# Product with the values: every second round, two units in a row, instead of every round

## The chip, the cores and the metric

The kernel runs on one core of one Trainium2 chip. The metric is the device time of one execution in microseconds. TensorE (PE) does the matrix products and loads their weights (PEld), VectorE (DVE) reduces and copies, ScalarE (ACT) does the exponentials and copies, GpSimd (POOL) does elementwise work in SBUF only, and SyncE (SP) starts DMAs. Products land in PSUM, which has eight banks of 128 x 512 f32.

## The reference

One transformer block with adaptive layer norm, for 2048 tokens of 256 features: latent attention with 16 heads, then eight experts of which each token uses two. Cut to the part that matters here:

```python
q = _rms_norm(x @ w_qa, q_a_norm_w) @ w_qb                 # 16 heads of 128 + 64
c_kv, k_rope = kv[..., :64], kv[..., 64:]                  # latent keys and values
scores = einsum('bhsd,bhtd->bhst', q_full, k_full) * scale
scores = where(tril, scores, min)
attn = softmax(scores)
out = einsum('bhst,bhtd->bhsd', attn, v)                   # the product with the values
x = x + ga * (out @ w_o)
h = _layernorm(x) * (1 + cb) + sb
x = x + gb * experts(h)                                    # top 2 of 8
```

## The kernel before

The program has three stages: `prepare` (weights, keys, latent values), `attend` (attention) and `experts`. The change is in `attend` alone.

**Tiling.** An *item* is one head and one group of 512 query rows (16 heads x 4 groups = 64 items). Group g sees g+1 blocks of 512 keys. A *unit* is two key tiles of 128 of one item. An item of group g has 2g full units and then two diagonal ones: the first (`d` = 0, an even unit number) and the second (`d` = 2, an odd number), of which only the part under the diagonal is computed. Every item has an even number of units and so starts at an even one. There are 320 units; 96 of the odd ones are full, 64 are diagonal. Of each pair of heads the groups come in the order 3, 1, 2, 0, so that the pattern of the work repeats every 40 units.

**Banks.** Scores of a unit go to one of two pairs of banks (`s_pair`), turn by turn. Three banks (`work_bank`) take, turn by turn, the small jobs of `WORK_ORDER`: row maxima of the scores ("max", L849, read by DVE in L782 or L779), the spread of an item's maxima over all partitions ("shift", L856, read by ACT in L706), and three query products for each pair of items ("q", parts 0 to 2, L837, read by ACT in L692 and by DVE in L757 to L770). A job waits until the one three before it has been read. One bank (`o_bank`) collects the product with the values of an item, and DVE copies it out once for each item (L808).

**Order.** Every engine has the same loop over rounds, r = -13 to 321, written out by hand, and does its instructions strictly in that order. Semaphores are all that ties the engines together. In round r:

- PE: scores of unit r (L876, six f32 products, with two bf16 mask products L867 ahead of them on a diagonal unit) with the maxima of later items between the halves (L849), then a shift (L856) in some odd rounds, a query product (L837) in some, and then the product with the values, `weigh(r - 2)`: up to 24 small 16-bit products (L891, L893, L895).
- ACT: exponentials of unit r (L726, or L730 twice on a diagonal one), a shift copy, the *seed* of unit r+2 (L717: the shift written to the scores' banks, on which the scores accumulate), a query copy (L692), or in part 2 the query's high part (L699), which waits for DVE's sums.
- DVE: maxima, an item's maximum and its spread (L787, L792), the turn of the queries (L757 to L770), the seed of the second diagonal unit (L800), and the copy of an item's output (L808).
- POOL: the low part of the exponentials (L669, L675), and of the queries (L661).

The scores of unit r wait for its seed, and the seed for the exponentials of unit r-2, which had the same banks. The exponentials of unit u wait until unit u-4 has been weighed, since `pt` has four slots. The first unit of an item waits in `weigh` for the copy of the item before (`o_seen`).

Of the kernel before, what the change touches and what calls it, by code (L numbers as in the profile page):

```python
# [56 lines left out]
UNITS = []  # L57
# [48 lines left out]
def seen_by(n):  # L106

    use = WORK_ORDER[n]
    return {"max": "v", "shift": "a", "q": "va"}[use[0]] if use[0] != "q" or use[2] < 2 else ""


SEEN = {e: [0, *itertools.accumulate(e in seen_by(n) for n in range(len(WORK_ORDER)))] for e in "av"}


def live(u, half):
# [5 lines left out]
def seed_on_vector(u):  # L121

    return UNITS[u][2] == 2
# [452 lines left out]
def attend(nc, sb, sem, k):  # L576
# [7 lines left out]
    with ExitStack() as own:  # L584
# [32 lines left out]
        def wait_seen(eng, n):  # L617
# [4 lines left out]
            for e in seen_by(n):  # L622
                eng.wait_ge(work_seen[e], SEEN[e][n + 1])

# [5 lines left out]
        with nc.Block() as block:  # L630
# [116 lines left out]
            def _(dve):  # L747
# [25 lines left out]
                def maximum(c):  # L773
                    item, t, part, n = CHUNKS[c]
                    w = WORK[("max", c)]
                    dve.wait_ge(work_done, w + 1)
                    of, to = work_of(w)[:, 0:n * P], mx[:, item % MAXIMA, t, part:part + 1]
                    if part == ITEMS[item][1]:
                        dve.tensor_tensor_reduce(out=of, in0=of, in1=mask16[:, BW - n * P:], scale=1.0, scalar=LOWEST, op0=ALU.add,  # L779
                                                 op1=ALU.max, accum_out=to).then_inc(work_seen["v"], 1)  # L780
                    else:
                        dve.tensor_reduce(out=to, in_=of, axis=AXX, op=ALU.max).then_inc(work_seen["v"], 1)  # L782
# [20 lines left out]
                def evacuate(u):  # L803
                    item, _, d = UNITS[u]
                    hp, g, h = ITEMS[item]
                    head = 2 * hp + h
                    dve.wait_ge(pv_done, u + 1)
                    dve.tensor_copy(lat[:, BT * g:BT * g + BT, head * (KVL + 1):head * (KVL + 1) + KVL + 1],  # L808
                                    o_bank[:, 0:BT * (KVL + 1)].rearrange("p (t n) -> p t n", t=BT)).then_inc(o_seen, 1)

                for r in ROUNDS:
                    for c in CHUNKS_AT[r]:
                        maximum(c)
                    if r in ITEM_MAX_AT:
                        item_shift(ITEM_MAX_AT[r])
                    p, part = PREP_AT.get(r, (0, 4))
                    if part < 3:
                        query_turn(p, part)
                    if 0 <= r + 2 < NU and seed_on_vector(r + 2):
                        seed(r + 2)  # L820
                    if r >= 2 and UNITS[r - 2][2] == 2:
                        evacuate(r - 2)

            @block.tensor
            def _(pe):
# [53 lines left out]
                def weigh(u):  # L879
                    item, j, d = UNITS[u]  # L880
                    at = u % PT_RING
                    if u == FIRST_UNIT[item] and item > 0:
                        pe.wait_ge(o_seen, item)
                    for half in range(2):
                        pe.wait_ge(low_ok, OPS[u + 1] - (0 if d is None or half else 1))
                        for t in range(0 if d is None else d + half, BT):
                            to = o_bank[:, t * (KVL + 1):t * (KVL + 1) + KVL + 1]
                            mine = slice(t * P, t * P + P)
                            end = d is not None and t == d + half
                            low_values, with_one = values[:, j + half, 0:KVL], values[:, j + half, KVL:2 * KVL + 1]  # L890
                            pe.matmul(to, cut(pt[:, at, half, mine]), with_one, start=(u == FIRST_UNIT[item] and half == 0 and t == 0),  # L891
                                      stop=False, skip_group_check=True)
                            pe.matmul(to[:, 0:KVL], cut(pt[:, at, half, mine]), low_values, start=False, stop=False,  # L893
                                      skip_group_check=True)
                            last = pe.matmul(to, pt_lo[:, at, half, mine], with_one, start=False, stop=end, skip_group_check=True)  # L895
                    last.then_inc(pv_done, 1)
# [6 lines left out]
                for r in ROUNDS:  # L903
                    for half in range(2):
                        if 0 <= r < NU:
                            scores(r, half)
                        for c in chunks_at(r, half):
                            maximum(c)
                    if r in SHIFT_AT:
                        shift_rows(SHIFT_AT[r])  # L910
                    p, part = PREP_AT.get(r, (0, 3))
                    if part < 3:
                        query_products(p, part)
                    if r >= 2:
                        weigh(r - 2)


def cut(a):

    return a.bitcast(BF16).rearrange("p (n e) -> p n e", e=2)[:, :, 1]  # L920
# [512 lines left out]
```

## Time and profile before

| | |
|---|---|
| median of 3 runs | 1254.86 us (1247.85 to 1255.21) |
| profiled execution | 1254.86 us, span 1253.1 us |
| attention in it | from about 116 to 991 us of the span |
| busy share of the span | PE 91%, PEld 77%, DVE 68%, ACT 63%, POOL 55% |
| mean granted TensorE clock | 0.956 |

PE is the busiest engine and the chain that ended last runs over it. Its busy time in the profile is modelled, since matmuls overlap: what one costs is read from the distance between two starts, not from its duration. The granted clock was 1.0 from 146 to 992 us of the span, nearly the whole of the attention.

### The profile page before, as it was taken

Reading aid. Unit: us, or ns where it says so; the run is one execution under the profiler, and the core shown is the slowest. Engines: PE = TensorE matmul, PEld = TensorE weight load, DVE = VectorE, ACT = ScalarE, POOL = GpSimd, SP = SyncE. Lnnn points to the kernel's source line nnn. Section 1 sums busy time; section 2 is a strip of 40 time slices with the busy share of each in tenths; the row PEclk is TensorE's granted clock in tenths of the full one; section 3 lists DMA queues with packets and bytes.
Section 4 is the critical chain, followed back from the end, with each engine's and each line's share of the span. In section 5 each row is a group of like instructions: output and inputs, shape, how many; then the busy total and the mean of one; then the engine's idle time right before and its main releaser. Section 6 shows DMA issues by size and latency. Waiting matters only on the chain. (4 is left out here: it accounts for less than half of the span.)

```text
span 1253.1 us, 27841 instructions
## 1 busy us (share of the span) xinstructions
PE 1146.3 (91%) x11372; PEld 958.8 (77%) x11372; DVE 846.8 (68%) x1900; ACT 787.5 (63%) x1166; POOL 690.3 (55%) x569
## 2 busy tenths in 40 slices
PE   2856899999999999999999999999999778989897
PEld 1744577888888888888888888888887667888886
DVE  2632876677676776777777677776675576767676
ACT  1254577777777878777787787877777532322222
POOL 0022366777777768686787776877777711202000
PEclk9876699999999999999999999999999879989998
DMA  9301110000100200100020020010000310000000
GB/s 277 95 1 48 29 44 18 2 18 25 38 19 2 62 2 19 44 19 19 2 62 18 2 61 2 19 44 19 18 2 1 114 57 1 1 18 1 18 18 17
DMA packets 57695, 39.91 MB, mean 32 GB/s; under 512 B 7744, under 2 KB 57152, under 8 KB 57408
## 3 DMA queue, kind: packets, MB, share of 16 engines
q1 hardware_dynamic: 51216, 33.94, 9.2%
q10 hardware_dynamic: 6352, 4.19, 1.4%
q8 instruction: 90, 1.47, 0.5%
q14 instruction: 37, 0.30, 0.1%
HBM read 33.66 MB, written 4.46 MB: 30 GB/s over the span
## 5 line engine op out<-in xcount | busy, mean ns | idle before, releaser
L669 POOL TENSOR_TENSOR pt_lo<-pt 128x1024 f16<-128x1024 f32 x192 | 370.5, 1939 | 181.5 <-ACT pt L726 181.2
L782 DVE TENSOR_REDUCE gates<-bank 128x1 f32<-128x512 f32 x384 | 261.6, 689 | 148.0 <-PE bank L849 145.1
L717 ACT ACTIVATE pair<-shift 128x1024 f32<-128x1024 f32 x256 | 263.7, 1030 | 12.2 <-ACT pt L730 0.4
L726 ACT ACTIVATE pt<-pair 128x1024 f32<-128x1024 f32 x192 | 196.2, 1022 | 108.3 <-PE pair L876 107.7
L891 PEld LDWEIGHTS bank<-values,pt 128*128 128x128 bf16 x2176 | 196.8, 98 | 80.1 <-issue 52.6
L891 PE MATMUL bank<-values,pt 128*128 128x65 f16 x2176 | 235.2, 194 | 6.0 <-DVE lat L808 5.1
L893 PE MATMUL bank<-values,pt 128*128 128x64 f16 x2176 | 231.8, 192 | 0.0
L895 PE MATMUL bank<-values,pt_lo 128*128 128x65 f16 x2176 | 230.8, 194 | 0.0
L675 POOL TENSOR_TENSOR pt_lo<-pt 128x512 f16<-128x512 f32 (+3 forms) x256 | 178.3, 722 | 45.0 <-ACT pt L730 44.9
L893 PEld LDWEIGHTS bank<-values,pt 128*128 128x128 bf16 x2176 | 202.0, 98 | 0.0
L895 PEld LDWEIGHTS bank<-values,pt_lo 128*128 128x128 f16 x2176 | 201.3, 97 | 0.0
L779 DVE CUSTOM_DVE_ANT_0 bank<-bank,mask 128x128 f32<-128x128 f32 (+3 forms) x256 | 126.1, 498 | 53.8 <-PE bank L849 48.7
L730 ACT ACTIVATE pt<-pair 128x512 f32<-128x512 f32 (+3 forms) x256 | 110.4, 437 | 45.7 <-PE pair L876 32.1
L876 PE MATMUL pair<-q_hi,kt_a_hi 128*128 128x512 f32 (+1 forms) x320 | 131.1, 410 | 0.0
L876 PE MATMUL pair<-q_hi,kt_b_hi 128*128 128x512 f32 (+1 forms) x320 | 130.5, 408 | 0.0
L849 PE MATMUL bank<-kt_a_hi,q_hi 128*128 128x512 f32 (+2 forms) x320 | 118.6, 375 | 3.4 <-DVE qf L757 1.6
L849 PE MATMUL bank<-kt_b_hi,q_hi 128*128 128x512 f32 (+2 forms) x320 | 117.4, 369 | 0.7 <-DVE gates L779 0.6
L876 PE MATMUL pair<-q_lo,kt_a_hi 128*128 128x512 f32 (+1 forms) x320 | 117.2, 366 | 0.0
L876 PE MATMUL pair<-q_hi,kt_a_lo 128*128 128x512 f32 (+1 forms) x320 | 117.2, 366 | 0.0
L876 PE MATMUL pair<-q_hi,kt_b_lo 128*128 128x512 f32 (+1 forms) x320 | 117.1, 366 | 0.0
L876 PE MATMUL pair<-q_lo,kt_b_hi 128*128 128x512 f32 (+1 forms) x320 | 116.6, 364 | 0.0
L661 POOL TENSOR_TENSOR q_lo<-qf,q_hi 128x512 fp32r<-128x512 f32 x64 | 84.4, 1340 | 19.6 <-ACT q_hi L699 18.1
(218 smaller groups left out, 2380.0 us busy)
## 6 DMA issues: line engine op xcount, KB each, us to landing
turn_by<-rope_cos_by_feature SPq DMA_DIRECT2D x64, 128.0 KB, 3.0
turn_by<-rope_sin_by_feature SPq DMA_DIRECT2D x64, 128.0 KB, 3.0
xs<-in_L_attn_x ACTq DMA_DIRECT2D x1, 2048.0 KB, 25.5
lat<-in_L_attn_w_o SPq DMA_DIRECT2D x1, 2048.0 KB, 26.6
xs_again<-in_L_attn_x SPq DMA_DIRECT2D x1, 2048.0 KB, 8.1
out<-xs_again SPq DMA_DIRECT2D x4, 512.0 KB, 2.8
lat<-in_L_wmod SPq DMA_DIRECT2D x1, 1536.0 KB, 16.3
lat<-in_L_attn_w_qb SPq DMA_DIRECT2D x1, 1152.0 KB, 8.0
```

The source lines that it names most:

```text
L669: pool.tensor_tensor(out=pt_lo[:, at].rearrange("p a n -> p (a n)"), in0=full, in1=cut(full), op=ALU.subtract).then_inc(low_ok, 1)
L675: pool.tensor_tensor(out=pt_lo[:, at, half, live(u, half):], in0=full, in1=cut(full), op=ALU.subtract).then_inc(low_ok, 1)
L717: act.activation(s_pair[u % 2][:, :, :], shift[:, item % SHIFTS:item % SHIFTS + 1, :].to_broadcast([P, 2, BW]), ACT.Copy).then_inc(seeded[ ...
L726: act.activation(pt[:, at], s_pair[u % 2][:, :, :], ACT.Exp).then_inc(exp_done, 1)
L730: act.activation(pt[:, at, half, live(u, half):], s_pair[u % 2][:, half, live(u, half):], ACT.Exp).then_inc(exp_done, 1)
L779: dve.tensor_tensor_reduce(out=of, in0=of, in1=mask16[:, BW - n * P:], scale=1.0, scalar=LOWEST, op0=ALU.add, op1=ALU.max, accum_out=to).t ...
L782: dve.tensor_reduce(out=to, in_=of, axis=AXX, op=ALU.max).then_inc(work_seen["v"], 1)
L849: pe.matmul(work_of(w)[:, 0:cols], q, kt_hi[h][:, part * BW:part * BW + cols], start=True, stop=True).then_inc(work_done, 1)
L876: last = pe.matmul(to, keys[a], q[b], start=False, stop=(m == 2), skip_group_check=True)
L891: pe.matmul(to, cut(pt[:, at, half, mine]), with_one, start=(u == FIRST_UNIT[item] and half == 0 and t == 0), stop=False, skip_group_check ...
L893: pe.matmul(to[:, 0:KVL], cut(pt[:, at, half, mine]), low_values, start=False, stop=False, skip_group_check=True)
L895: last = pe.matmul(to, pt_lo[:, at, half, mine], with_one, start=False, stop=end, skip_group_check=True)
```

## The change

`weigh` is no longer called once in every round. Even rounds have none; an odd round r has two in a row, of units r-3 and r-2. So an odd unit is weighed in the round in which it was weighed before, and an even unit one round later. DVE's copy of an item's output belongs to the odd units and stays in its round. The same instructions run, on the same banks: three for the small jobs, one for the output.

```diff
+def values_due(r):
+
+    return (r - 3, r - 2) if r >= 3 and r % 2 else ()
...
             @block.vector
...
-                    if r >= 2 and UNITS[r - 2][2] == 2:
-                        evacuate(r - 2)
+                    for u in values_due(r):
+                        if UNITS[u][2] == 2:
+                            evacuate(u)
...
             @block.tensor
...
-                    if r >= 2:
-                        weigh(r - 2)
+                    for u in values_due(r):
+                        weigh(u)
```

PE at the end of an even round that holds a query product, and what follows it (a line number of the changed kernel is 6 higher than the same line before). Before:

```order
2453 L837 MATMUL bank<-ql_hi,wq_pair_hi 128x512 [waits work_seen_a,wq_in]
2454 L837 MATMUL bank<-ql_lo,wq_pair_hi 128x512
2455 L837 MATMUL bank<-ql_hi,wq_pair_lo 128x512
2456 L891 MATMUL bank<-values,pt 128x65 [waits low_ok,o_seen]
2457 L893 MATMUL bank<-values,pt 128x64
2458 L895 MATMUL bank<-values,pt_lo 128x65
2459 L891 MATMUL bank<-values,pt 128x65
```

In the changed kernel, at the same place:

```order
2453 L843 MATMUL bank<-ql_hi,wq_pair_hi 128x512 [waits work_seen_a,wq_in]
2454 L843 MATMUL bank<-ql_lo,wq_pair_hi 128x512
2455 L843 MATMUL bank<-ql_hi,wq_pair_lo 128x512
2456 L873 MATMUL pair<-ident,mask 128x128 [waits seeded_v]
2457 L873 MATMUL pair<-ident,mask 128x128
2458 L882 MATMUL pair<-q_hi,kt_b_hi 128x256
```

The 21 value products (L891, L893, L895) that stood between the query product and the next unit's scores are gone from there; the odd round's scores, its maxima and its own query product come that much sooner after the even round's. They stand, with the 9 of the odd unit behind them, after the odd round's query product:

```order
2466 L843 MATMUL bank<-ql_hi,wq_pair_hi 128x512 [waits work_seen_a,work_seen_v]
2467 L843 MATMUL bank<-ql_lo,wq_pair_hi 128x512
2468 L843 MATMUL bank<-ql_hi,wq_pair_lo 128x512
2469 L897 MATMUL bank<-values,pt 128x65 [waits low_ok,o_seen]
2470 L899 MATMUL bank<-values,pt 128x64
2471 L901 MATMUL bank<-values,pt_lo 128x65
```

The second place is the start of an odd full unit, three rounds behind another query product (a part 2). Before, its first product follows value products:

```order
2829 L891 MATMUL bank<-values,pt 128x65
2830 L893 MATMUL bank<-values,pt 128x64
2831 L895 MATMUL bank<-values,pt_lo 128x65
2832 L876 MATMUL pair<-q_hi,kt_b_hi 128x512 [waits seeded_a]
2833 L876 MATMUL pair<-q_lo,kt_b_hi 128x512
```

In the changed kernel it follows a maximum, and nothing stands between it and the even round's jobs:

```order
2806 L882 MATMUL pair<-q_hi,kt_b_lo 128x512
2807 L855 MATMUL bank<-kt_b_hi,q_hi 128x384 [waits work_seen_v]
2808 L882 MATMUL pair<-q_hi,kt_b_hi 128x512 [waits seeded_a]
2809 L882 MATMUL pair<-q_lo,kt_b_hi 128x512
```

What moved in both is only the block of value products; the order of all else on PE is as it was.

## Rows read from the trace of the kernel before

**Rows 1.** The page, part 1: busy time, share of the span, instructions

```profile
PE 1146.3 (91%) x11372; PEld 958.8 (77%) x11372; DVE 846.8 (68%) x1900; ACT 787.5 (63%) x1166; POOL 690.3 (55%) x569
```

**Rows 2.** Stretches, us: busy us (instructions) of PE, PEld, DVE, ACT, POOL; clock; DMA

```profile
146.00:200.00 54.00, 51.21 (x541) 41.23 (x540) 42.62 (x90) 39.95 (x56) 36.62 (x34) 1.00 0.09 26
200.00:942.00 742.00, 741.48 (x8542) 610.96 (x8543) 532.27 (x1126) 587.92 (x777) 551.57 (x443) 1.00 0.08 23
942.00:990.00 48.00, 43.21 (x560) 35.86 (x558) 26.29 (x51) 33.75 (x50) 35.04 (x32) 1.00 0.01 1
```

**Rows 3.** Timeline, PE around the value products of a full unit: start us, duration us

```profile
495.33 0.40 PE L849 MATMUL bank<-kt_b_hi,q_hi 128*128 128x512 f32 x1
...
495.56 0.21 PE L891 MATMUL bank<-values,pt 128*128 128x65 f16 x1
...
496.31 0.47 PE L876 MATMUL pair<-q_hi,kt_b_hi 128*128 128x512 f32 x1
...
496.62 0.39 PE L876 MATMUL pair<-q_lo,kt_b_hi 128*128 128x512 f32 x1
```

**Rows 4.** Groups, 200 to 950 us: count | busy us, mean ns | idle before

```profile
L891 PE MATMUL bank<-values,pt 128*128 128x65 f16 x1948 | 210.4, 194 | 2.0 <-DVE lat L808 1.6
...
L699 ACT ACTIVATE q_hi<-qf 128x512 fp32r<-128x512 f32 x54 | 34.1, 633 | 9.8 <-DVE qf L770 9.2
```

**Rows 5.** Waits of PEld, 200 to 950 us: total us, times, longest us

```profile
PEld bank L891 <- DVE lat L808: 4.6, 8, 2.0
```

**Rows 6.** Waits of PE, 942 to 990 us

```profile
PE bank L891 <- DVE lat L808: 3.6, 3, 1.8
PE pair L867 <- DVE pair L800: 1.0, 1, 1.0
```

**Rows 7.** Timeline from a query product 0 to part 1

```profile
408.25 0.21 PE L891 MATMUL bank<-values,pt 128*128 128x65 f16 x1
...
408.99 0.27 PE L867 MATMUL pair<-ident,mask 128*128 128x128 bf16 x2
...
409.05 0.58 ACT L692 ACTIVATE qf<-bank 64x512 f32<-64x512 f32 x1
...
410.20 0.39 PE L837 MATMUL bank<-ql_hi,wq_pair_hi 96*128 96x512 f32 x1
```

**Rows 8.** Timeline from a query product 2 to the shift behind it

```profile
414.17 0.21 PE L891 MATMUL bank<-values,pt 128*128 128x65 f16 x1
...
414.82 0.48 PE L876 MATMUL pair<-q_hi,kt_b_hi 128*128 128x512 f32 x1
...
415.20 1.41 DVE L770 TENSOR_TENSOR qf<-bank,qf 64x512 f32<-64x512 f32 x2
...
416.75 0.41 PE L856 MATMUL bank<-spread,ones_r 128*128 128x512 f32 x1
```

**Rows 9.** Timeline: a query part 2 on ACT, the seed behind it

```profile
382.55 0.21 PE L891 MATMUL bank<-values,pt 128*128 128x65 f16 x1
...
383.20 0.48 PE L876 MATMUL pair<-q_hi,kt_b_hi 128*128 128x512 f32 x1
...
384.36 1.29 ACT L699 ACTIVATE q_hi<-qf 128x512 fp32r<-128x512 f32 x2 [0.29 <-DVE qf L770]
...
385.56 1.01 ACT L726 ACTIVATE pt<-pair 128x1024 f32<-128x1024 f32 x1
...
386.60 1.03 ACT L717 ACTIVATE pair<-shift 128x1024 f32<-128x1024 f32 x1
...
387.19 0.21 PE L891 MATMUL bank<-values,pt 128*128 128x65 f16 x1
...
387.93 0.48 PE L876 MATMUL pair<-q_hi,kt_b_hi 128*128 128x512 f32 x1
```

**Rows 10.** Timeline: a seed on ACT and its unit, at another place of the pattern

```profile
429.78 1.03 ACT L717 ACTIVATE pair<-shift 128x1024 f32<-128x1024 f32 x1
...
431.23 0.48 PE L876 MATMUL pair<-q_hi,kt_a_hi 128*128 128x512 f32 x1
```

## The prediction

> **What bounds the kernel now.** I read the busy shares first, then the stretches, the waits of PE, and last the timeline around the places where the change moves work. PE is busiest with 91% [rows 1], but its durations overlap. The stretches say more: from 200 to 942 us, three fifths of the span, PE is busy for 741.48 of 742 us at a granted clock of 1.00, which is the upper of its two levels, 2.4 GHz; ACT is busy for 79% of it, POOL for 74%, DVE for 72% [rows 2]. So PE sets the pace there with hardly a wait, and the others follow with some slack. What the change is worth is what it does to PE's row of starts: something taken out of it is gained, any wait put into it is lost in full.
>
> **The change, part by part.**
>
> *Fewer changes between f32 and 16-bit products.* Around a block of 24 value products the starts are: a maximum at 495.33, the first value product at 495.56, the next unit's scores at 496.31 and 496.62 [rows 3]. An f32 product of 512 columns holds up the next start by 0.23 us. The first one behind the block holds the next up for 0.31 us, so leaving the block costs 0.08 us. The block takes 0.75 us; its 24 products at the 194 ns of their group [rows 4] would make 4.7 us, so durations say nothing, and the pitch is about 31 ns. The start of the block is slow by some 0.03 us (I take the later products of the block at 30 ns: 24 x 30 is 0.72). Each separate block thus costs 0.11 us. Where is one saved? An odd full unit now follows a maximum or a query product, f32 behind f32: 96 times. At the 64 odd diagonal units it is not: their two bf16 mask products stand first, so there was one 16-bit run from the value products to the masks, and now there are the masks alone with the same change on either side. 96 x 0.11 = **10.5 us less**.
>
> *The copy of the output.* The first value product of an item waits until DVE has copied the item before. From 200 to 950 us the weight loads waited for it 8 times, 4.6 us in all, of which the loads would have waited about 0.2 each for their turn: 3 us [rows 5], 1.6 of it shown at the product itself [rows 4]. At the end of the attention, where little else fills PE, it is 3.6 us in 3 waits, and 1.0 us for a seed [rows 6]. The pair of units never straddles two items, and between the last of an item and the first of the next stand now the scores of two units, not of one, some 2 us more: longer than the longest wait, 2.0. I take the 3 us as gained and half of the 4.6 us at the end, since the same late DVE delays a seed or a query there next: **5.3 us less** (bounds: 0 and 7.6).
>
> *What the moved block used to cover.* This is the other side. In an even round the block gave ACT and DVE 0.65 to 0.75 us (21 or 24 products) between the even round's jobs and the odd unit. ACT's and DVE's work of the even round starts when PE's scores and jobs of that round are done, and does not come sooner; PE's odd unit does, by the block and, if full, by the 0.08 us. Two rounds together are as long as before, so what depends on the odd round two back keeps its distance, and what even rounds need from odd ones gains room. Losses are only where odd work needs something of the even round before it (or three before), with less slack than 0.65 to 0.83 us. From the timeline, with 0.06 us for a semaphore (an estimate between 0.03, from 386.57 to 386.60 on one engine [rows 9], and 0.14, from 416.61 to 416.75 [rows 8]):
>
> 1. Query product 1 waits until the bank of product 0 is read. ACT's copy ends at 409.05 + 0.58 = 409.63; product 1 starts at 410.20 [rows 7]. It would start 0.74 us sooner (408.99 - 408.25), at 409.46, and waits until 409.69: 0.23 us. The other three places of the pattern have 0 to 0.1 us more slack; mean 0.17. There are 27 preparations of queries from 200 to 950 us (54 high parts, two for each [rows 4]): 4.6 us.
> 2. The shift that follows a query part 2 needs DVE's sums: these end at 415.20 + 1.41 = 416.61, the shift starts at 416.75 [rows 8]. It would start 0.65 + 0.08 us sooner, at 416.02: 0.65 us of wait. This meets one preparation in four: 4.4 us.
> 3. The seed behind a part 2 is the dear one. ACT has to do the high parts (384.36 to 385.6), the exponentials of the odd unit (385.56), and only then the seed of the odd unit after it, 386.60 + 1.03 = 387.63; that unit starts at 387.93 [rows 9]. In the changed order its start lies one block and one change earlier (the block at 387.19 to 387.93 comes behind it, and the change at 383.20 is gone): 387.93 - 0.74 - 0.08 = 387.11 against 387.69, a wait of 0.6 us. At two more places of the pattern the seed ends at 429.78 + 1.03 = 430.81 for a start at 431.23 [rows 10], 0.42 us of slack instead of 0.30, and the wait is 0.46; the fourth has an odd diagonal unit there, whose seed is DVE's and has slack. Mean 0.51 at three of four preparations, 20 times: 10.3 us.
>
> Together **19.3 us more**. Bounds: 0, if ACT and DVE had been held up by PE's odd rounds more than I read; and twice as much, 39 us, if each wait makes the next engine late again.
>
> *Before 200 us.* Here DVE has three maxima in most rounds and PE is busy for 51.21 of 54 us [rows 2]. In the six odd rounds the jobs come 0.7 us sooner to a DVE that is already late: between 0 and 4 us more. I take **1 us**, near the lower end, since DVE itself loses nothing. The clock is 1.00 from 146 us on; the block moved before that changes a round or two.
>
> *POOL, DMAs, DVE's order.* No DMA moves. Value products of even units come a round later, those of odd units at the same place, so POOL's low parts are never later than needed. The exponentials of unit u wait for the value products of u-4: these now stand at the end of the odd round before, ahead of the scores that the exponentials need anyway. Nothing added.
>
> Sum: -10.5 - 5.3 + 19.3 + 1 = +4.5 us. The profiled execution took 1254.86 us, 1.8 us over its span, and is itself the median of the three: **1259 us**. The three runs lie within 0.6%, so I count less than 1% (12.5 us) as no change that could be told.
>
> **A rule weighed against the trace.** The rows put a load and its value product at 31 ns, in runs of at most 26 with the masks. The Trainium skill (TensorE: Matmul & The Clock Gate, Back-to-back issue gap) gives about 81 ns for each load with its product of 128 columns in a sustained stream. This trace does not agree for its 65 columns: a block of 24 would take 1.9 us, and took 0.75. By the page's figure every wait above would grow by some 1.2 us, and 54 of them would make the sum about +69 us, an estimate from that page that I do not use.
>
> **The rivals.**
>
> - *The waits do not appear* (0.17). For it: ACT and DVE are busy for under 80%, and an odd round gives back what an even one takes. Against: the three chains hang on even rounds and were followed instruction by instruction. Then -10.5 - 5.3: 1239 us.
> - *The lateness carries on* (0.13). For it: ACT has 0.6 us of slack in a mean round (154 us [rows 2] over some 270 rounds, ten for each preparation), and the high parts alone take 1.3. A late seed makes late exponentials, a late shift, and a late seed again. Against: the odd round is 0.7 us longer than it was and lets ACT catch up. Twice the waits: 1259 + 19 = 1278 us, slower. It decides from 28 us of waits on, 1.4 times my sum, where the slowdown passes 1%.
> - *Long runs of small products starve* (0.08). PE now does 48 loads and products in a row at 96 places; the longest run in these rows is 26. All that is shown is that the supply of instructions makes 742 us / 8542 = 87 ns for a pair on average [rows 2] and 31 ns in short runs, for which a stock may have been filled during the long f32 products. If it could do only the average, the 22 pairs beyond 26 cost 22 x 56 ns = 1.2 us each time: +118 us, 1377 us; anything between is possible. The Trainium skill (the same page, its table) has a queue of 64 for TensorE, 32 pairs, by which 16 pairs would run dry: 86 us instead of 118 if the supply had only that average. No row here shows a queue's depth.
> - *Part of the waits* (0.10): half of them, 1249 us.
>
> My forecast has 0.52: its own range, from the bounds of the single terms, is 1250 to 1268.
>
> **How the numbers follow.** Faster by over 1% needs under 1242.3: the first rival and a little of the fourth, 0.18. Slower by over 1% needs over 1267.4: the second and third rival and 0.04 of the forecast's own range, 0.25. Within 1%: 0.57. The range reaches from the first rival to the second, 1236 to 1279, and leaves out the starving one, half of the second and a third of the first: 0.2.
>
> **What would show it.** Right: 96 of the 0.31 us distances behind 16-bit products are gone; PE's starts show waits for ACT's seed (L717) before odd full units three rounds behind a query part 2, for DVE's sums before a shift, and short ones before query product 1; the waits for L808 are gone; and PE's busy share from 200 to 942 us falls from 99.9% to about 97.5%. Wrong: if the distance between value products grows in the second half of a run of 48, the third rival holds; if no wait of PE shows at these places and the stretch to 942 us ends more than 5 us sooner, the waits did not come; if DVE or ACT have waits on each other in rounds without a query, lateness carries on.

## The result, and the profile after

| | before | changed |
|---|---|---|
| median, us (8 runs each) | 1254.58 | 1261.17 |
| lowest to highest, us | 1247.85 to 1256.13 | 1258.15 to 1265.1 |
| profiled execution: time, span, us | 1254.86, 1253.1 | 1260.55, 1258.8 |

The ratio is 1.0064 [1.0042, 1.0086]: slower by 0.6%, or 6.6 us, less than the 1% that the prediction counted as no change. Forecast were 1259 us, in a range of 1236 to 1279.

The page of the changed kernel, part 1, and then its stretches (columns as in [rows 2]). Lines of PE stand 6 further down than before, those of the other engines 5: the scores are L882, the value products L897 to L901, the shift L862, the query products L843, ACT's seed L722, its high parts L704, DVE's query sums L775, its copy of the output L813.

```profile
PE 1144.1 (91%) x11372; PEld 959.2 (76%) x11372; DVE 859.0 (68%) x1900; ACT 772.5 (61%) x1166; POOL 700.7 (56%) x569
```

```profile
146.00:200.00 54.00, 52.48 (x561) 42.99 (x561) 43.64 (x93) 39.98 (x56) 38.44 (x33) 1.00 0.09 26
200.00:942.00 742.00, 727.69 (x8320) 601.17 (x8317) 534.98 (x1097) 562.42 (x761) 549.41 (x433) 1.00 0.08 22
942.00:990.00 48.00, 47.28 (x581) 39.70 (x580) 32.06 (x70) 37.46 (x50) 36.44 (x30) 1.00 0.01 2
```

Beside [rows 1] nothing shows: all shares are within 2 points. Beside [rows 2] it does. In the long stretch PE was busy for 741.48 of 742 us and is now for 727.69: 98.1% against 99.9%, and 8320 products fit where 8542 did. Before 200 us and behind 942 us it is busier than it was (52.48 for 51.21, 47.28 for 43.21 us; the attention now ends 10 us later, so the last window holds somewhat other work). The waits of PE from 200 to 942 us name the cause (line <- what it waited for: us in all, times, longest):

```profile
PE pair L882 <- ACT pair L722: 8.2, 20, 0.5
PE bank L862 <- DVE qf L775: 2.9, 6, 0.5
PE bank L843 <- DVE qf L762: 0.7, 2, 0.4
PE bank L843 <- DVE gates L787: 0.4, 1, 0.4
```

These are the places of the forecast: 20 waits for a seed, 6 for the sums before a shift, and the three longest of those before query product 1. The view counts only gaps over 0.15 us, and counts them from the modelled end of the product before, so its sum of 12.2 us is too low; the distances between starts, below, give the full price and show a wait at all 27 query products 1. The wait for the copy of the output is gone from here. At the end of the attention, 942 to 1000 us, it is gone too; in place of 4.6 us in [rows 6] stand 0.7:

```profile
PE bank L897 <- POOL pt_lo L674: 0.4, 1, 0.4
PE pair L873 <- DVE pair L805: 0.3, 1, 0.3
```

One such wait closely, at the place of [rows 9]. First ACT and then PE of the changed kernel (start us, duration us):

```profile
385.69 1.29 ACT L704 ACTIVATE q_hi<-qf 128x512 fp32r<-128x512 f32 x2 [0.30 <-PE pair L882]
386.88 1.01 ACT L731 ACTIVATE pt<-pair 128x1024 f32<-128x1024 f32 x1
387.92 1.03 ACT L722 ACTIVATE pair<-shift 128x1024 f32<-128x1024 f32 x1
...
383.64 0.39 PE L843 MATMUL bank<-ql_hi,wq_pair_lo 96*128 96x512 f32 x1
383.87 0.40 PE L882 MATMUL pair<-q_hi,kt_b_hi 128*128 128x512 f32 x1
384.11 0.39 PE L882 MATMUL pair<-q_lo,kt_b_hi 128*128 128x512 f32 x1
...
388.24 0.34 PE L855 MATMUL bank<-kt_b_hi,q_hi 128*128 128x384 f32 x1
389.01 0.50 PE L882 MATMUL pair<-q_hi,kt_b_hi 128*128 128x512 f32 x1 [0.43 <-ACT pair L722]
389.35 0.39 PE L882 MATMUL pair<-q_lo,kt_b_hi 128*128 128x512 f32 x1
```

ACT still does high parts, exponentials and seed in this order, and the seed ends at 387.92 + 1.03 = 388.95. A maximum of 384 columns holds up the next start by 0.17 us, so the scores could have started at 388.41; they start at 389.01. The wait is 0.60 us, as forecast. Two more things are to be seen. At 383.87 the odd unit follows a query product, f32 behind f32, and the next start comes 0.24 us later and not 0.31: the saved change. And behind the wait the next start comes after 0.34 us and not 0.23: the wait costs 0.11 us more than itself. That was in no term.

### The profile page after: what moved, and what is told of

It is laid out like the page before. It is cut to its first block and busy times, and to the rows that moved or that the text cites. A ratio compares the mean times of both kernels' runs of the same rounds, so it can differ in the third digit from the quotient of the medians.

```text
span 1258.8 us, 27841 instructions
## 1 busy us (share of the span) xinstructions
PE 1144.1 (91%) x11372; PEld 959.2 (76%) x11372; DVE 859.0 (68%) x1900; ACT 772.5 (61%) x1166; POOL 700.7 (56%) x569
## 3 DMA queue, kind: packets, MB, share of 16 engines
q8 instruction: 90, 1.47, 0.5%
## 5 line engine op out<-in xcount | busy, mean ns | idle before, releaser
L787 DVE TENSOR_REDUCE gates<-bank 128x1 f32<-128x512 f32 x384 | 263.2, 690 | 138.0 <-PE bank L855 130.9
L722 ACT ACTIVATE pair<-shift 128x1024 f32<-128x1024 f32 x256 | 263.5, 1029 | 12.2 <-ACT pt L735 0.4
L897 PEld LDWEIGHTS bank<-values,pt 128*128 128x128 bf16 x2176 | 197.5, 98 | 35.3 <-issue 33.5
L897 PE MATMUL bank<-values,pt 128*128 128x65 f16 x2176 | 216.9, 193 | 0.9 <-DVE lat L813 0.5
L899 PE MATMUL bank<-values,pt 128*128 128x64 f16 x2176 | 215.2, 192 | 0.0
L901 PE MATMUL bank<-values,pt_lo 128*128 128x65 f16 x2176 | 214.6, 194 | 0.0
L680 POOL TENSOR_TENSOR pt_lo<-pt 128x512 f16<-128x512 f32 (+3 forms) x256 | 185.0, 747 | 53.0 <-ACT pt L735 52.4
L901 PEld LDWEIGHTS bank<-values,pt_lo 128*128 128x128 f16 x2176 | 199.8, 97 | 0.0
L735 ACT ACTIVATE pt<-pair 128x512 f32<-128x512 f32 (+3 forms) x256 | 103.5, 431 | 64.6 <-PE pair L882 59.5
L882 PE MATMUL pair<-q_hi,kt_a_hi 128*128 128x512 f32 (+1 forms) x320 | 128.6, 402 | 5.6 <-ACT pair L722 5.6
L882 PE MATMUL pair<-q_hi,kt_b_hi 128*128 128x512 f32 (+1 forms) x320 | 127.4, 398 | 2.6 <-ACT pair L722 2.6
L882 PE MATMUL pair<-q_hi,kt_a_lo 128*128 128x512 f32 (+1 forms) x320 | 117.4, 367 | 0.0
L882 PE MATMUL pair<-q_lo,kt_a_hi 128*128 128x512 f32 (+1 forms) x320 | 117.1, 366 | 0.0
L882 PE MATMUL pair<-q_hi,kt_b_lo 128*128 128x512 f32 (+1 forms) x320 | 117.1, 366 | 0.0
L882 PE MATMUL pair<-q_lo,kt_b_hi 128*128 128x512 f32 (+1 forms) x320 | 116.7, 365 | 0.0
```

The lines of the kernel that those rows point to most:

```text
L680: pool.tensor_tensor(out=pt_lo[:, at, half, live(u, half):], in0=full, in1=cut(full), op=ALU.subtract).then_inc(low_ok, 1)
L722: act.activation(s_pair[u % 2][:, :, :], shift[:, item % SHIFTS:item % SHIFTS + 1, :].to_broadcast([P, 2, BW]), ACT.Copy).then_inc(seeded[ ...
L735: act.activation(pt[:, at, half, live(u, half):], s_pair[u % 2][:, half, live(u, half):], ACT.Exp).then_inc(exp_done, 1)
L882: last = pe.matmul(to, keys[a], q[b], start=False, stop=(m == 2), skip_group_check=True)
```

## Where the time went

To add this up I took all starts of attention work on PE from unit 40 to unit 240, five patterns of 40 units, and split the distances: the 0.232 us of a product of 512 columns (0.174 for 384, 0.117 for 256, 0.03 for a value product); 0.085 for the first f32 product behind a 16-bit run; what lies inside a value block; and each distance over 0.05 us that is left, as a wait (with the slower start behind it). The 0.085 is a mean too: behind value products or masks the first product of 512 columns holds up the next start by 0.317 us in every kernel here, against 0.232. In us, all kernels of this document:

| kernel | total | changes to f32 | waits | unit 319 starts at | from there to the end |
|---|---|---|---|---|---|
| before | 528.5 | 17.0 (200) | 1.2 | 987.2 | 265.9 |
| changed | 543.2 | 11.9 (140) | 21.7 | 997.6 | 261.2 |
| e1, e2, e3 | 539.5, 535.7, 532.7 | 13.6, 11.9, 13.6 | 15.8, 14.2, 9.0 | 991.0, 988.5, 984.4 | 263.2, 266.4, 263.9 |
| e4, e5 | 535.1, 548.0 | 11.9, 17.0 | 13.6, 20.9 | 985.9, 1015.1 | 265.7, 263.4 |
| e6, e7 | 576.0, 579.2 | 34.0, 11.9 | 27.7, 55.9 | 1068.7, 1073.3 | 260.1, 265.8 |
| e8, e9 | 533.8, 525.2 | 13.2, 13.6 | 10.8, 1.7 | 987.2, 976.2 | 266.4, 266.5 |
| e10, e11, e12 | 535.5, 530.1, 523.3 | 11.9, 12.3, 12.3 | 13.9, 8.0, 1.3 | 986.3, 981.2, 972.4 | 265.9, 262.9, 266.2 |

From before to changed the 200 units took 14.7 us more: 20.5 more waits, 5.1 less for 60 changes and 1.3 less inside the blocks (together 0.107 us for each saved change; 0.6 us is left over). Up to unit 40 the changed kernel gains 2.0 us (252.1 and 250.1), behind unit 240 another 2.3 (206.6 and 204.3). So unit 319 starts 10.4 us later. Of the 2.0 us, 0.9 lie before the first unit (141.6 and 140.7 us), where no values are weighed yet; over all kernels here it starts between 139.1 and 142.5 us, so this is luck, and the attention itself costs 11.3 us. The rest of the program, which is the same code in both, took 4.7 us less, and that is no merit of the change. The stretches behind the attention, of before, of the changed kernel and of e9:

```profile
991.00:1253.10 262.10, 222.69 (x1376) 200.92 (x1376) 182.98 (x441) 75.09 (x119) 41.69 (x27) 0.91 0.09 29
```

```profile
1001.60:1258.80 257.20, 217.07 (x1376) 195.61 (x1376) 182.82 (x442) 75.14 (x119) 41.77 (x27) 0.94 0.09 29
```

```profile
980.20:1242.70 262.50, 222.71 (x1376) 201.00 (x1376) 182.99 (x442) 75.09 (x119) 41.74 (x27) 0.91 0.09 29
```

All three do the same 1376 products; DVE, ACT and POOL are busy for the same time to 0.2 us, and only PE is not. The column that differs is the granted clock, 0.94 against 0.91: PE was at the lower level, 1.2 GHz, for 31.7 us there, and for 49.0 (before) and 49.1 (e9). The runs of the changed kernel bear it out: five had a mean clock of 0.961 to 0.964 and took 1258.15 to 1261.8 us, three had 0.956 or 0.957, as before's profile, and took 1263.6 to 1265.1. Over the other kernels the end follows the clock too, but not it alone: it took 260.1 us with 28.2 us at the lower level (e6) and 266.5 with 49.1 (e9), yet 265.7 and 263.4 with 42.5 and 42.4 (e4, e5). With equal clocks the change thus costs 9 to 10 us, near what the attention says; the 6.6 of the medians hold some luck. For this reason the experiments are judged by the attention first.

## The experiments

My theory was: the block of value products gave three chains of ACT and DVE their cover, and each wait comes from the loss of one place of it. Against it stood that the waits come from lateness that is handed on (then putting one place back mends more than its place), and that PE loses something in long runs of small products. e1 to e4 and e7 to e12 start from the changed kernel, e5 and e6 from the one before. e1, e2, e3, e8 and e9 replace the rule of rounds by a table: units for which COND holds have their values in the round of before (one change to f32 more if the odd unit behind is a full one, none if it is diagonal), all others stay paired:

```
-    return (r - 3, r - 2) if r >= 3 and r % 2 else ()
+VALUES_ROUND = {u: u + 2 if u % 2 or COND else u + 3 for u in range(NU)}
+    return [u for u in (r - 3, r - 2) if VALUES_ROUND.get(u) == r]
```

### e1: the values put back in the round of a query part 2

```
COND: PREP_AT.get(u + 2, (0, 3))[1] == 2
```

> The changed kernel, but in the 32 even rounds that hold a query part 2 the value products stay as they were (one unit there, one in the odd round behind). My theory (waits of what hangs on even rounds): the waits for the seed three rounds behind a part 2 (0.47, 0.60 and 0.70 us per 40 units, with 0.11 each to start again) and the one before the shift (0.64 + 0.11) go, 2.85 us per 40 units; 4 of the 12 saved changes from 16-bit to f32 come back, 0.44 us. Net 2.4 us x 6.75 = 16 us less than the changed kernel: about 1245 us. Rival 1 (long runs of small products are slow by themselves): 27 of 96 runs of 48 are halved, so about a quarter of the 17 us of unexplained loss goes, 1257 us. Rival 2 (ACT and DVE are late everywhere once rounds are uneven): waits move to other rounds, no change, 1259 to 1261 us.

Measured: 1260.19 us, 1.0048 [1.0031, 1.0064] against before. The waits of PE, 200 to 942 us:

```profile
PE pair L885 <- ACT pair L725: 6.1, 19, 0.4
PE bank L846 <- DVE gates L790: 0.4, 1, 0.4
```

A miss, and it taught the geometry. The wait before the shift is gone (this block stands right ahead of it), but the seed waits are still there (0.37, 0.49 and 0.61 us at their three places, about 0.11 less than in the changed kernel, since the saved change came back). The seed that ACT does after the high parts belongs to the unit three rounds behind part 2, and the block that covered it is the one of the round before that unit, not that of part 2.

### e2 and e3: the values put back in the round of part 0, and of parts 0 and 2

```
COND of e2: PREP_AT.get(u + 2, (0, 3))[1] == 0
COND of e3: PREP_AT.get(u + 2, (0, 3))[1] in (0, 2)
```

> The changed kernel, but in the 32 even rounds that hold a query product 0 the value products stay as they were. My theory: the waits before query product 1 go (0.24, 0.28, 0.19 to 0.59, 0.27 us per 40 units, with 0.08 each to start again), 1.4 us per 40 units; no change from 16-bit to f32 comes back, since the odd unit behind each of these rounds is a diagonal one. 9 us less than the changed kernel: about 1252 us. Rival 1 (long runs): the pairs at these places are the short ones of diagonal units or of a full unit and a diagonal one, so nothing or 1 us. Rival 2 (lateness everywhere): no change.

> The changed kernel with the value products of one unit left in all 64 even rounds that hold a query part 0 or 2. If the two kinds of waits are apart, their gains add: 16 + 9 = 25 us less than the changed kernel, 1236 us, and 1.4% less than the kernel before: what is left of the change is 8 saved changes per 40 units (7 us in all) and the waits for the copy of the output that are gone (3 us, and up to 8 at the end of the attention). If lateness merely moves (rival 2): 1250 us or more, and waits for the seed at other places in the trace.

Measured: e2 1257.08 us, 1.0029 [1.0014, 1.0043]; e3 1252.22 us, 0.9988 [0.9976, 1.0001]. The waits of e2, and then those of e3:

```profile
PE pair L885 <- ACT pair L725: 8.2, 20, 0.6
PE bank L865 <- DVE qf L778: 2.9, 6, 0.5
```

```profile
PE pair L885 <- ACT pair L725: 6.1, 19, 0.4
```

Each block put back takes away its own wait: query product 1 in e2, that and the shift in e3. e2 gains what was forecast, 9.1 us in the attention (997.6 - 988.5; 9 were expected); in the time only 4, since its end is 5.2 us longer than the changed kernel's short one. e3 gains 13.2 of the 25 expected: the seeds keep their waits, some 12 us (0.37, 0.49 and 0.60 in 40 units, and the starts behind them, 6.75 times). No place mends another, which speaks against lateness that is handed on.

### e4 and e5: another distance of the preparations, with and without the pairing

```
-AHEAD, PREP_AHEAD = 5, 6
+AHEAD, PREP_AHEAD = 5, 5
```

> The changed kernel, with every preparation of queries one round later, so that parts 0 and 2 fall into odd rounds, which have two units of value products behind them, and part 1 into an even one. My theory: the waits for the seed and before query product 1 go (they hang on rounds that are long now), and a wait of 0.25 to 0.35 us comes before query product 2 or the shift in the same round, since these now hang on the even round of product 1: -29 + 9 us, 1241 us. Rival 2 (lateness everywhere): no change, 1261 us. A preparation that is one round later for its readers costs nothing if the first maxima of an item had more than 3 us of slack, and shows as a wait for q_hi if not.

> The kernel before, with every preparation of queries one round later: the control for the fourth run. In it all rounds have their value products, so nothing should depend on whether a query part is in an even or an odd round: no change by my theory, 1253 to 1257 us. If it were faster by itself, the gain of the fourth run would not be one of the pairing.

Measured: e4 1253.42 us, 0.9992 [0.9975, 1.001]; e5 1280.49 us, 1.0205 [1.0184, 1.0226]. The waits of e4, and then those of e5:

```profile
PE bank L843 <- ACT qf L697: 6.2, 20, 0.4
PE bank L862 <- issue: 1.4, 6, 0.2
PE pair L873 <- DVE pair L805: 1.3, 6, 0.2
```

```profile
PE bank L891 <- DVE lat L808: 23.1, 26, 1.6
PE pair L867 <- ACT pair L717: 2.1, 1, 2.1
```

With the jobs of queries moved by a round the seed waits are gone and waits before query product 2 stand in their place: the cost of the pairing sits where jobs and missing blocks meet, not in the pairing itself. e4 misses its 1241 us: its new waits (0.37 to 0.54 us before three of the four query products 2, 0.40 before a shift, 0.37 before a diagonal unit) come to 13.6 us in 200 units, where the 0.25 to 0.35 us of the forecast made 9 in the whole attention. The control e5 was expected to change nothing and is 26 us slower: it brings 26 waits for the copy of the output, which e4 does not have. So here the pairing is worth 27 us (1280.49 - 1253.42). 10.3 of it are the saved changes. The waits are the rest: counted in starts up to unit 319, e5 has 39.7 us, 31.9 of them for value products, and e4 has 23.0, none for value products. The term that the prediction sized at 5.3 is worth some 32 here: its size hangs on how late DVE is where an item ends.

### e6: more changes to f32, without moving anything across rounds

The block of before is cut in two: its first half follows the first chunk of scores' maxima of the same round, its second stays.

```
 for half in range(2):
     ...
+    if half == 0 and r >= 2:
+        weigh(r - 2, 0)
...
-weigh(r - 2)
+weigh(r - 2, 1)
```

> The kernel before, with the value products of each unit in two blocks, that of the first key tile between the two halves of the next scores and that of the second where all were: twice as many blocks, the same products. It measures what a change from f32 to 16-bit and back costs. My theory, 0.11 us for each additional block (0.08 to leave it, 0.03 to start it): 320 x 0.11 = 35 us more, 1290 us, and up to 5 more for waits on the copy of the output, which comes 1 us sooner. If changes cost nothing and the 0.31 us after a block were hidden elsewhere: no change.

Measured: 1330.75 us, 1.0625 [1.0594, 1.0655]; its waits are for L808 (23.2 us) and POOL's low parts (1.8 us). The table has the answer to what it was made for: 200 blocks more cost 17.0 us of changes and 2.3 within the blocks, 0.097 us each, against 0.107 saved by the change and 0.11 forecast. The time misses its 1290 us by 41 through the waits, of which at most 5 were expected. Of its 47.5 us more in that stretch 26.5 are waits: half of each block now comes a part of a round sooner, nearer to the copy of the output.

### e7: the pair in even rounds

```
-    return (r - 3, r - 2) if r >= 3 and r % 2 else ()
+    return [u for u in ((r - 3, r - 2) if r % 2 == 0 else (r - 2,) if r == NU + 1 else ()) if 0 <= u < NU]
```

> The changed kernel with the pairs in even rounds: units r-3 (odd) and r-2 (even) in an even round, so that the odd rounds are the short ones and each second pair or so straddles two items. My theory: the seeds and the first query product no longer wait (they hang on even rounds, now long); query product 2, or a shift, waits 0.3 us behind the odd round of product 1 (27 times, 8 us); the changes saved are those before even full units, 10.5 us; and at the 63 starts of an item the copy of the output stands between two blocks in a row with nothing to cover it, 0.42 us of copy and some 0.2 for the semaphores, 40 us, more where DVE is late. 1254.6 - 10.5 + 8 + 40 = 1292 us. If the copy's wait were hidden, 1252 us.

Measured: 1340.07 us, 1.0682 [1.0658, 1.0705]. Its only wait of PE from 200 to 942 us, and one case of it on DVE and PE:

```profile
PE bank L897 <- DVE lat L813: 56.8, 49, 2.9
...
501.02 0.42 DVE L813 COPY lat<-bank 128x260 f32<-128x260 f32 x1
...
501.50 0.20 PE L897 MATMUL bank<-values,pt 128*128 128x65 f16 x1 [0.83 <-DVE lat L813]
```

Now a pair straddles two items: its odd unit ends one, its even unit begins the next, and between them PE can do nothing but wait for the copy from the single output bank, 0.9 to 1.7 us and once 2.5 in a pattern. All waits for seeds, shifts and queries are gone, so the same saved changes come with other waits, two and a half times as long (55.9 us against 21.7 in 200 units). The forecast of 1292 us had the place right and the price too low: 0.6 us for each of 63 copies, 40 us, where the 62 waits up to unit 319 sum to 86. This is what the odd rounds of the change avoid.

### e8 and e9: the block ahead of the late seed put back, and all three places

```
COND of e8: PREP_AT.get(u, (0, 3))[1] == 2
COND of e9: that of e8, or that of e2, or (u + 3 in SHIFT_AT and that of e1)
```

> The first run left the waits for the seed where they were, because it put back the wrong block: a seed behind a query part 2 in round r is waited for by unit r+3, and what no longer stands ahead of that is the value block of unit r, in round r+2. Here that block, and no other, stays in its old round (32 of them). My theory: the three waits for the seed go (0.48, 0.60, 0.70 us per 40 units and 0.11 each to start again), three saved changes come back (0.3 us), all other waits stay: 1.8 us x 6.75 = 12 us less than the changed kernel, 1249 us. Two of the first units of items are among the blocks, so the 0.23 us for the copy of the output may be back once per 40 units. Rival (a late ACT shows wherever rounds are uneven): the waits for the seed move to another unit and the time stays at 1258 to 1261 us.

> The changed kernel with one value block left in its old round at each place where a wait was found: in rounds with a query product 0, in the round two behind a part 2, and in that of a part 2 with a shift behind it. My theory: no waits are left from unit 40 to 240 but 0.23 us per 40 units for the copy of the output, 8 of 12 changes stay saved: 3.7 us less per 40 units than the changed kernel, 25 us in all, 1236 us; 1.4% faster than the kernel before, where 7 us are the changes, and the rest the waits for the copy of the output and the end of the attention. Rival: 1250 us as in the third run.

Measured: e8 1254.35 us, 0.9999 [0.9991, 1.0008]; e9 1243.96 us, 0.9921 [0.9909, 0.9934]. The waits of e8, and then those of e9:

```profile
PE bank L865 <- DVE qf L778: 2.9, 6, 0.5
PE bank L900 <- DVE lat L816: 1.1, 6, 0.2
PE bank L846 <- DVE gates L790: 0.4, 1, 0.4
```

```profile
PE bank L900 <- DVE lat L816: 1.1, 6, 0.2
```

This settles the seed: with the right block put back all 20 waits are gone. e8 takes 9.4 us less than the changed kernel over 200 units (1.9 for 40, where 1.8 were expected). In e9 nearly everything is gone: over 200 units it takes 18.0 us less than the changed kernel (3.6 for 40 units, where 3.7 were expected), and beats before by 3.3 through changes to f32 alone. Both times miss what was expected, 1249 and 1236 us, by 5 and 8 us. Most of that is the changed kernel's short end, from which they were counted: e8's attention is 10.4 us shorter and its end 5.2 longer, e9's attention 21.4 shorter (25 were expected) and its end 5.3 longer, at the clock shown above.

### e10 and e11: the high and low parts a round later

ACT's high parts and POOL's low parts of a query go from the round of part 2 into the one behind it, after ACT's seed; e11 has also the blocks of e9 for query product 1 and the shift.

```
-p, part = PREP_AT.get(r, (0, 3))
-if part == 2:
+p, part = PREP_AT.get(r, (0, 4))
+if part == 3:
```

> The changed kernel with the cause taken away and not the cover put back: ACT makes the high part of the queries (and POOL the low part) a round later, in an odd round, which has the long stretch of value products behind it. My theory: the waits for the seed go and no saved change comes back: 2.1 us per 40 units, 14 us less than the changed kernel, 1247 us; the waits before query product 1 and the shift stay. If the waits came from the missing cover as such and not from ACT's chain in even rounds: no change. A wait for q_hi before the first maximum of an item would show that the high part is now too late.

> The tenth run with one value block left in its old round where a query product 0 stands, and where a shift follows a part 2. No waits from unit 40 to 240, 11 of 12 changes saved: 4.2 us less per 40 units than the changed kernel, 28 us, 1233 us, the fastest of all, 1.7% under the kernel before. If the gain of 0.11 us for a saved change were an artefact of the trace, this run and the ninth would be alike and both near 1240 us.

Measured: e10 1254.29 us, 0.9996 [0.9984, 1.0008]; e11 1245.5 us, 0.9927 [0.9915, 0.994]. The waits of e10; then e11's only wait of PE, and the job on DVE on which it hangs:

```profile
PE bank L862 <- DVE qf L775: 2.9, 6, 0.5
PE bank L843 <- DVE qf L762: 2.6, 6, 0.7
PE bank L843 <- DVE gates L787: 0.4, 1, 0.4
```

```profile
PE bank L846 <- DVE qf L765: 6.3, 6, 1.3
...
525.13 0.69 DVE L765 TENSOR_TENSOR qf<-bank,turn_by 64x512 f32<-64x512 f32 x1 [2.32 <-POOL q_lo L669]
```

The seed waits are gone without giving up a saved change: it was the order on ACT that made them. Yet e10 gains 1.5 us in 40 units and not 2.1, and 6.9 in the time where 14 were expected: at one place the wait before query product 1 grew from 0.19 us in most cases to 0.55 and more, and 0.15 came before a shift. In e11, from which 1233 us and no waits were expected, the next preparation follows closely at one place of the pattern, DVE must wait for POOL's late low parts, and PE for DVE, 1.17 us and 0.10 for the start behind it.

### e12: late only where the late seed belongs to a full unit

```
+LATE = {p for p, r in enumerate(PREP_ROUND) if 0 <= r + 5 < NU and UNITS[r + 5][2] is None and r % 2 == 0}
-if part == 2:
+if part == (3 if p in LATE else 2):
```

The rest is e11.

> The eleventh run with the queries' high and low parts a round later only where the odd unit three rounds behind part 2 is a full one (three of four preparations); the fourth, which the next preparation follows after 4 rounds, keeps its round. In the eleventh run POOL's low part there ended only when the next preparation's first turn was waiting for it: 1.17 + 0.10 us per 40 units on PE. My theory: that wait goes, 0.25 us before a shift stays, and the 3 changes that the ninth run gave back stay saved: from unit 40 to 240 about 1.3 us per 40 units less than the eleventh, 523.7 us in all against 525.2 of the ninth. Time 1241 to 1244 us. If a saved change is worth less than 0.11 us in the time, it is no faster than the ninth run.

Measured: **1241.21 us**, 0.9896 [0.988, 0.9913] against before, the fastest of all. From unit 40 to 240 it takes 523.3 us, where 523.7 were expected. That is 1.9 less than e9, which has 15 changes to f32 more (1.6 us at 0.107), so a saved change keeps its price; the medians differ by 2.8 us. Its long stretch:

```profile
200.00:930.00 730.00, 730.00 (x8481) 612.65 (x8478) 558.48 (x1119) 572.24 (x775) 554.16 (x442) 1.00 0.08 23
```

PE is busy for all of it (but for 0.15 us before a shift, once in a pattern, which is below the view's limit), and the place of [rows 9] now looks so on ACT and PE:

```profile
380.37 1.03 ACT L726 ACTIVATE pair<-shift 128x1024 f32<-128x1024 f32 x1
381.34 1.14 ACT L708 ACTIVATE q_hi<-qf 128x512 fp32r<-128x512 f32 x2
...
381.81 0.34 PE L859 MATMUL bank<-kt_b_hi,q_hi 128*128 128x384 f32 x1
381.98 0.39 PE L886 MATMUL pair<-q_hi,kt_b_hi 128*128 128x512 f32 x1
```

The seed ends at 381.40, ahead of the scores at 381.98, and the high parts come behind it; nothing waits.

## Why the prediction was right

*The changes to f32* (-10.5 us). Right: 0.107 us for each in the changed kernel, 0.097 in e6, against 0.11; 96 x 0.107 is 10.3.

*The copy of the output* (-5.3 us). Right within its bounds and low: it is 7.1 us. Up to 950 us the starts lose 3.2 us to it before (1.75 at the product that starts at 200.08 us, the 1.6 of [rows 4], and six times 0.23), where 3 was taken, and nothing in the changed kernel. Of the 4.6 us at the end 3.9 went, where half was taken: nothing delayed a seed next. e7 shows why it works (the pair does not straddle items), e4 against e5 that it may be worth 32 us.

*The waits* (+19.3 us) are the step that was mis-sized; places, order and cause were right. For 40 units, in us:

| | forecast | measured |
|---|---|---|
| seeds, three places | 0.60 + 0.46 + 0.46 = 1.52 | 0.60 + 0.47 + 0.70 = 1.77 |
| shift | 0.65 | 0.64 |
| query product 1, four places | 0.68 | 1.17 |
| slower start behind each of the 8 waits | 0 | 0.75 |
| sum | 2.85 | 4.34 |

From 200 to 950 us that is 6.75 patterns: 29.3 us and not 19.3; added up wait by wait it is 28.0. Half of the miss is the start behind a wait. The seed at the place of [rows 10] was 0.23 us longer since before there was a wait for the copy of the output on the same way, shorter than the view of waits shows at PE; its gain was spent at once on waiting for the seed. And query product 1 waits 0.46 to 0.59 us in three of its twenty cases, where the view names DVE and not ACT as the last to be ready (0.19 us of the 0.49 in the table); the other 0.3 are places that had less slack than was read.

*Before 200 us* (+1 us). Right in sign, and 0.5 us: the waits of PE from unit 4 to 9, where the jobs come sooner, sum to 1.1 us before and 1.6 in the changed kernel.

The terms as measured add up to the attention: -10.3 - 7.1 + 28.0 + 0.5 = +11.1 us, against 11.3 with equal starts and 10.4 as profiled. The sum had +4.5. The end behind it gave 4.7 back in the profiled execution, and the time, 1261, lies closer to 1259 than the terms deserve: the waits were sized 9 to 10 us too low, the gain at the copy 2 us too low, and the short end hid much of the rest. The prediction's own range, 1250 to 1268, held the time, but it does not follow from the bounds that were named for the terms, which reach from 1237 to 1287 us.

*The rivals.* That the waits do not appear fell with the list of waits. Lateness is not carried on: e1, e2, e3 and e8 each take away the waits of their places and leave the others within 0.11 us, but for the three odd cases of query product 1. It does happen where two preparations follow closely: e10 and e11 lengthen a wait before query product 1 that they do not touch. The starving of long runs is refuted; the run of 48 pairs behind the wait shown above, first, 24th, 25th and last product, and the scores behind it:

```profile
390.97 0.21 PE L897 MATMUL bank<-values,pt 128*128 128x65 f16 x1
...
391.68 0.20 PE L901 MATMUL bank<-values,pt_lo 128*128 128x65 f16 x1
391.72 0.19 PE L897 MATMUL bank<-values,pt 128*128 128x65 f16 x1
...
392.41 0.20 PE L901 MATMUL bank<-values,pt_lo 128*128 128x65 f16 x1
392.44 0.47 PE L882 MATMUL pair<-q_hi,kt_b_hi 128*128 128x512 f32 x1
```

The first 24 take 0.75 us, the next 24 take 0.72. The Trainium skill (TensorE: Matmul & The Clock Gate, Back-to-back issue gap) gives 81 ns for each load with its product of 128 columns. Taken over to these products of 65 columns, as an estimate from that page, these 48 would take 3.9 us. They took 1.47, and the measurement decides. The same page, in its table, has a queue of 64 for TensorE. 48 pairs are 96 instructions, and no gap appeared; no run shows what the queue held.

## What to carry to other kernels

A block of work that costs the bounding engine nothing to move may still be the cover of somebody else's chain: before moving it, follow for each chain which round's block stands between its end and who needs it, and write the slack beside it, place by place of the pattern. Merge blocks where the slack is larger than the block and leave them apart where it is not (e9), or reorder the short jobs on the helping engine so that what the bounding engine needs next comes first (e12): both keep most of the gain and lose the waits. And when two versions differ by half a per cent, compare them up to a point behind which they are the same code.

## What the runs showed of the hardware

- After PE has waited for a semaphore, the start behind the first f32 product of 512 columns comes late: 0.34 us and not 0.23 behind a seed's wait or in a shift, 0.31 in a query product (0.33 and 0.34 behind two of its longest waits). That is 0.11 us and 0.07 to 0.08. Eight short waits in a pattern thus cost 3.6 us by themselves and 0.75 for the starts.
- A pair of a weight load and a 16-bit product of 65 columns keeps its 30 ns over at least 48 pairs.
- The same work behind the attention took 257 us with 31.7 us at the lower clock level and 262 with 49.0; 5 us, 0.4% of the time, come and go with the clock.
- From unit 40 to unit 319 of e7 PE waited nine times for 2.5 us or more for the copy of the output, and the clock fell eight times, six times for 3.4 us and twice for 6.8. Each fall came during such a wait or at most 1.3 us behind it, five times in the middle of the dense work that followed it. Here is one, and the stretch behind it up to the next:

```profile
495.00:498.50 3.50, 3.50 (x12) 2.82 (x10) 0.75 (x2) 0.32 (x1) 1.46 (x2) 0.51 0.59 153
498.50:611.00 112.50, 103.34 (x1192) 86.03 (x1192) 77.42 (x163) 83.65 (x112) 76.93 (x63) 1.00 0.07 18
```

The clock column reads 0.51 and then 1.00. Waits of up to 1.7 us did not bring it down there, but a long wait does not always do it either: the one of these nine that ended at 844.05 us, and one of 3.0 us that ended at 206.77 left the clock at 1.00. A transfer of 153 GB/s ran at the moment of the fall above. It is no condition: of the next two rows of e7, the first stands behind the wait of 844.05, with a transfer of 180 GB/s and the clock at 1.00, and the second at the fall of 990 us, with no transfer and the clock at 0.50. In e6 too the clock fell for 3.4 us where a wait of 2.7 us ended (204.94 us), without a transfer.

```profile
845.00:848.00 3.00, 3.00 (x15) 2.46 (x14) 1.61 (x4) 1.30 (x2) 1.51 (x3) 1.00 0.62 180
990.50:993.50 3.00, 2.85 (x28) 2.56 (x29) 0.09 (x1) 0.42 (x1) 2.35 (x2) 0.50 0.00 0
```

And in the kernel before a transfer of 173 GB/s left the clock at 1.00. So the falls go with long waits of PE and not with transfers; why two of the long waits had none stays open:

```profile
470.00:473.00 3.00, 3.00 (x35) 2.42 (x34) 1.53 (x3) 2.94 (x4) 3.00 (x2) 1.00 0.61 173
```
